# Attention on one core: the inverse softmax sums applied to the probabilities, or to the product with the values

## The reference, cut to what matters

```
q = xn @ w_q.T        # 16 heads of 32
k, v = split(xn @ w_kv.T)             # one key and one value head, shared by the 16
attn = softmax(causal(rotary(q) @ rotary(k).T))
out = (attn @ v, heads side by side) @ w_proj.T + b_proj
shared = relu(xn @ up.T)**2 @ down.T  # 1024 wide
routed = 8 of 32 experts for each token, chosen by groups, weighed, summed
return x + out + shared + routed
```

## Time and profile before

| | |
|---|---|
| median of 3 runs | 1771.65 us (1771.54 to 1773.84) |
| span of the profiled execution | 1784.5 us |
| PE busy of the span | 1640.6 us, 92% |
| DVE busy of the span | 1202.6 us, 67% |
| ACT busy of the span | 1073.5 us, 60% |
| middle, batch 0 | 143.1 to 304.3 us |
| middle, batches 1 to 7 | 304.3 to 1125.4 us |
| experts | from about 1156 us |

### The profile page before, as it was taken

How to read it: one execution, slowest core, us unless ns; L and a number is a source line. 1 busy time by engine, 2 the same in 40 slices (tenths; PEclk the granted TensorE clock), 3 DMA queues, 4 the chain that set the end, 5 groups by cost and what they waited for, 6 DMA issues and landing times.

```text
span 1784.5 us, 40620 instructions
## 1 busy us (share of the span) xinstructions
PE 1640.6 (92%) x10811; PEld 1385.8 (78%) x10811; DVE 1202.6 (67%) x3666; ACT 1073.5 (60%) x2799; POOL 822.7 (46%) x669
## 2 busy tenths in 40 slices
PE   5836779999999999999999999899999999999999
PEld 5835557777777777777777777689999999999987
DVE  7857876877777867767778678355555555555567
ACT  2324545775675756757757667466666666666652
POOL 0032101442443424434424345177777777777760
PEclk9967889999999999999999999999999999999999
DMA  7983242443434434435434344489999999998894
GB/s 283 372 279 88 55 71 79 137 128 101 157 115 144 126 99 131 135 103 153 137 104 133 102 146 122 135 154 184 186 185 195 194 177 197 210 176 159 139 251 187
DMA packets 193666, 277.91 MB, mean 156 GB/s; under 512 B 37464, under 2 KB 133855, under 8 KB 190884
## 3 DMA queue, kind: packets, MB, share of 16 engines
q0 software_dynamic: 60352, 92.59, 23.9%
q1 hardware_dynamic: 78148, 117.20, 23.0%
q10 hardware_dynamic: 54944, 65.52, 12.5%
HBM read 123.93 MB, written 131.76 MB: 143 GB/s over the span
## 4 chain that ended last, share of the span: by engine, by line
PE 63%; DVE 12%; issue 8%; ACT 4%; DMA 3%; POOL 2%; DVEq 1%; SPq 0%; another core or an unknown queue 0%; ACTq 0%; POOLq 0%
PE e_psH L1644 12%; PE e_psY L1655 11%; PE m_psT L1250 6%; PE m_psU L64 4%; DVE m_sc L1047 4%; PE m_psU L66 4%; PE m_psS L1233 4%; PE m_psU L65 4%; PE m_psO L1274 4%; PE e_psX L1629 3%; PE m_psY L66 3%; PE m_psY L64 3%; PE m_psY L65 3%; POOL sums L1609 2%; ACT m_sc L899 2%
## 5 line engine op out<-in xcount | busy, mean ns | idle before, releaser
L1609 POOL DMA_INDIRECT sums<-e_y,e_where x287 | 445.3, 1551 | 156.5 <-issue 94.4
L823 POOL DMA_INDIRECT slot_rows<-m_row,slots x256 | 268.6, 1049 | 501.1 <-ACT m_sc L899 457.2
L899 ACT ACTIVATE m_sc<-m_sc,m_low 128x512 f32<-128x512 f32 (+3 forms) x512 | 283.7, 557 | 173.9 <-DVE m_low L1047 150.8
L1644 PE MATMUL e_psH<-e_xt,e_w_of 128*128 128x128 f32 x2296 | 303.6, 275 | 3.2 <-ACT e_xt L1504 3.2
L1047 DVE CUSTOM_DVE_ANT_0 m_sc<-m_psS,cst 128x512 f32<-128x512 f32 (+3 forms) x512 | 230.0, 485 | 107.0 <-PE m_psS L1233 104.8
L1655 PE MATMUL e_psY<-e_w,e_ht 128*128 x1148 | 295.7, 380 | 2.3 <-ACT e_ht L1515 2.1
L1644 PEld LDWEIGHTS e_psH<-e_xt,e_w_of 128*128 128x128 f32 x2296 | 279.0, 192 | 3.7 <-ACT e_xt L1504 3.5
L1510 ACT ACTIVATE e_w_of<-e_w 128x512 f32 x287 | 180.9, 630 | 120.9 <-issue 119.0
L1250 PE MATMUL m_psT<-cst,m_sc 128*128 128x128 f32 x1280 | 204.1, 280 | 10.5 <-ACT m_pt L910 9.4
L1655 PEld LDWEIGHTS e_psY<-e_w,e_ht 128*128 128x128 f32 x1148 | 196.2, 191 | 18.0 <-issue 3.2
L1233 PE MATMUL m_psS<-m_ks,m_qs 96*128 96x256 f32 (+2 forms) x512 | 156.6, 371 | 57.4 <-DVE m_low L1047 39.8
(11 more groups left out here) (204 smaller groups left out, 3166.1 us busy)
## 6 DMA issues: line engine op xcount, KB each, us to landing
e_row<-slot_rows ACTq DMA_DIRECT2D x287, 144.5 KB
m_qs<-m_qhi SPq DMA_DIRECT2D x256, 64.0 KB
e_w<-in_w SPq DMA_DIRECT2D x256, 64.0 KB
f_xt<-in_x SPq DMA_DIRECT2D x8, 1024.0 KB, 9.5
xnt_hi<-f_hi SPq DMA_DIRECT2D x8, 1024.0 KB, 4.5
xnt_lo<-f_lo SPq DMA_DIRECT2D x8, 1024.0 KB, 8.1
m_qs<-m_qlo SPq DMA_DIRECT2D x128, 64.0 KB
m_res<-in_x SPq DMA_DIRECT2D x8, 1024.0 KB
```

What stands on the lines that cost most here:

```text
L823: pool.indirect_dma_start(out=xs, out_offset=bass.IndirectOffsetOnAxis(ap=slots_sb[:, g, k:k + 1], axis=0), in_=row[g % 2][:, :], in_offse ...
L899: nc.scalar.activation(cols, cols, ACT.Exp, bias=low[:, h % 2, i:i + 1], scale=-1.0, accum_out=total[:, h % 2, i:i + 1]).then_inc(exp_done, 1)
L1609: pool.indirect_dma_start(out=both_sums, out_offset=bass.IndirectOffsetOnAxis(ap=where[u % NY][:, 0:1], axis=0), in_=y[u % NY][:, :], in_o ...
L1644: mm = pe.matmul(psH[u % 2][:, k * P:(k + 1) * P], w1_of[u % 2][:, c * INTER + k * P:c * INTER + (k + 1) * P], xt[u % 2][:, c * P:(c + 1) ...
```

## The change

The probabilities stay unscaled: `scale` keeps only its reciprocal (now `invert`), written so that the inverse sums of four heads lie side by side. Before a group's product with the values, DVE copies these inverses to the part of ot that the group will fill, each repeated over 32 columns (`spread`, 128x512, in slots 4, 8, 12 and 16, between the first two masks and the shared expert's step). PE turns them with four transposes into the bank psU (`inverses`, in slots 5, 9, 13 and 17, ahead of the third row of scores), so that they stand as the product with the values does. ACT copies them back to ot (`copy_inverses`, between its second and third exponentials). When the product is there, DVE multiplies it with them into ot (`normalise`, at the end of the same slot). ACT's `keep` goes; its last step, the high parts for the projection, becomes `highs`. The wait for `tagged_saved` stands now in `spread(1)`, on DVE in slot 8.

```diff
+INV_AT = {HC * _c + HC + 1: _c for _c in range(KC)}
...
-                def keep(c):
+                def copy_inverses(c):
+                    act.wait_ge(u_done, at(b, NU, U_AT[f"inv{c}"] + 1))
+                    nc.scalar.activation(ot[:, c, :], psU[:, :], ACT.Copy).then_inc(inv_copied, 1)
...
-                    if first and c == 1:
-                        act.wait_ge(routing.tagged_saved, 16)
...
-                        dve.wait_ge(scaled, at(b, NH, h - 1))
...
-                def scale(h):
+                def invert(h):
                     dve.wait_ge(exp_done, at(b, NH * TB, TB * (h + 1)))
-                    nc.vector.reciprocal(inv[:, h % 2, :], total[:, h % 2, :]).then_inc(inv_made, 1)
-                    dve.wait_ge(inv_made, at(b, NH, h + 1))
-                    for i in range(TB):
-                        cols = sc[:, h % 2, SPC[i]:SPC[i] + (i + 1) * P]
-                        last = nc.vector.tensor_scalar(cols, cols, inv[:, h % 2, i:i + 1], None, ALU.mult)
-                    last.then_inc(scaled, 1)
+                    nc.vector.reciprocal(inv[:, h // HC % 2, :, h % HC], total[:, h % 2, :]).then_inc(inv_made, 1)
+
+                def spread(c):
+                    dve.wait_ge(inv_made, at(b, NH, HC * (c + 1)))
+                    if first and c == 1:
+                        dve.wait_ge(routing.tagged_saved, 16)
+                    nc.vector.tensor_copy(ot[:, c, :].rearrange("p (k d) -> p k d", d=HD),
+                                          inv[:, c % 2, :, :].rearrange("p i n -> p (i n)").unsqueeze(2).broadcast_to([P, TB * HC, HD])
+                                          ).then_inc(inv_spread, 1)
+
+                def normalise(c):
+                    dve.wait_ge(pv_done, at(b, KC, c + 1))
+                    dve.wait_ge(inv_copied, at(b, KC, c + 1))
+                    nc.vector.tensor_tensor(ot[:, c, :], psO[:, :], ot[:, c, :], ALU.mult).then_inc(o_out, 1)
...
                         mask_and_min(s, ROWS[1])
+                    if s + 1 in INV_AT:
+                        spread(INV_AT[s + 1])
                     if 1 <= s <= NH:
                         shared(s - 1)
...
-                        scale(s)
+                        invert(s)
                     if s - 2 in Q_AT:
                         low_part(b, f"q{Q_AT[s - 2]}")
+                    if s in INV_AT:
+                        normalise(INV_AT[s])
...
                     if g == 0:
-                        pe.wait_ge(scaled, at(b, NH, h + 1))
+                        pe.wait_ge(exp_done, at(b, NH * TB, TB * (h + 1)))
...
+                def inverses(c):
+                    bank_free(b, f"inv{c}")
+                    pe.wait_ge(inv_spread, at(b, KC, c + 1))
+                    for i in range(TB):
+                        mm = pe.transpose(psU[:, i * P:(i + 1) * P], ot[:, c, i * P:(i + 1) * P], ident)
+                    mm.then_inc(u_done, 1)
...
+                    if s in INV_AT:
+                        inverses(INV_AT[s])
                     if s < NH:
                         scores(s, ROWS[2])
                         scores(s, ROWS[3])
```

More of the change, by code:

```diff
@@ L636 @@
 Q_AT = {q_slot(n): n for n in range(1, KC)}
+INV_AT = {HC * _c + HC + 1: _c for _c in range(KC)}
 U_ORDER = []
-for _s in range(NH):
-    U_ORDER.append(f"up{_s}")
+for _s in range(NSLOT):
+    if _s in INV_AT:
+        U_ORDER.append(f"inv{INV_AT[_s]}")
+    if _s < NH:
+        U_ORDER.append(f"up{_s}")
     if _s in Q_AT:
@@ L683, in middle @@
         total = sb("m_total", [P, 2, TB])
-        inv = sb("m_inv", [P, 2, TB])
+        inv = sb("m_inv", [P, 2, TB, HC])
         ot = ot_flat[:, :].rearrange("p (c s) -> p c s", c=KC)
@@ L712, in middle @@
         rot_step, rotated, lo_made, v_made = sem("m_rot_step"), sem("m_rotated"), sem("m_lo_made"), sem("m_v_made")
-        s_out, inv_made, scaled = sem("m_s_out"), sem("m_inv_made"), sem("m_scaled")
+        s_out, inv_made, inv_copied, inv_spread = sem("m_s_out"), sem("m_inv_made"), sem("m_inv_copied"), sem("m_inv_spread")
         sq_made, sqlo_made, res_made, y_out = sem("m_sq_made"), sem("m_sqlo_made"), sem("m_res_made"), sem("m_y_out")
@@ L852, in act_program @@
         def act_program(act, load_first_rows):
-            for s_ in (exp_done, relu_made, sqhi_made, ta_out, tb_out, o_out):
+            for s_ in (exp_done, relu_made, sqhi_made, ta_out, tb_out, inv_copied):
                 act.sem_inc(s_, BASE)
@@ L912, in ta, with highs @@
                         nc.scalar.activation(pt[:, h % HC, 1024:1280], psT[0][:, 0:256], ACT.Copy).then_inc(ta_out, 1)
-                def keep(c):
-                    act.wait_ge(pv_done, at(b, KC, c + 1))
-                    act.wait_ge(y_done, at(b, 4, 0))
-                    if first and c == 1:
-                        act.wait_ge(routing.tagged_saved, 16)
[L920 to L926, removed]
+                def copy_inverses(c):
+                    act.wait_ge(u_done, at(b, NU, U_AT[f"inv{c}"] + 1))
+                    nc.scalar.activation(ot[:, c, :], psU[:, :], ACT.Copy).then_inc(inv_copied, 1)
+                def highs():
+                    act.wait_ge(pv_done, at(b, KC, KC))
+                    act.wait_ge(y_done, at(b, 4, 0))
+                    for k in range(KC):
+                        act.wait_ge(o_out, at(b, KC, k + 1))
+                        nc.scalar.activation(oh[:, k, :], ot[:, k, :], ACT.Copy).then_inc(oh_made, 1)
                 def shared(s):
@@ L939, in batch @@
                     if s < NH:
-                        for i in ROWS:
-                            exps(s, i)
+                        exps(s, ROWS[0])
+                        exps(s, ROWS[1])
+                    if s in INV_AT:
+                        copy_inverses(INV_AT[s])
+                    if s < NH:
+                        exps(s, ROWS[2])
+                        exps(s, ROWS[3])
                     if s == 2 and not first:
@@ L947, in batch @@
                         shared(s)
-                    if s > HC and s % HC == 1:
-                        keep(s // HC - 1)
+                    if s == NSLOT - 1:
+                        highs()
                     if first and PROJ_AT <= s < PROJ_AT + KC:
@@ L988, in dve_program @@
             dve.sem_inc(v_made, BASE - 1)
-            for s_ in (s_out, inv_made, scaled, sq_made, sqlo_made, res_made, y_out):
+            for s_ in (s_out, inv_made, inv_spread, o_out, sq_made, sqlo_made, res_made, y_out):
                 dve.sem_inc(s_, BASE)
@@ L1119, in batch @@
                     dve.wait_ge(oh_made, b * KC + c + 1)
-                    nc.vector.tensor_tensor(ol[:, c, :], psO[:, :] if c == KC - 1 else ot[:, c, :], oh[:, c, :].bitcast(F32),
+                    nc.vector.tensor_tensor(ol[:, c, :], ot[:, c, :], oh[:, c, :].bitcast(F32),
                                             ALU.subtract).then_inc(ol_made, 1)
@@ L1165, in bank_free @@
                     pe.wait_ge(relu_made, at(b, NH, int(last[2:]) + 1))
+                elif last.startswith("inv"):
+                    pe.wait_ge(inv_copied, at(b, KC, int(last[3:]) + 1))
                 elif last == "vt":
```

## The result

The changed kernel takes 1797.95 us (median of 4 runs, 1796.38 to 1799.46), against 1772.74 for the kernel before (4 runs): the ratio is 1.014, interval 1.0126 to 1.0155, slower by 25 us. Forecast were 1800.0 us and +28.4.

What follows compares the result with a forecast made beforehand. PE was taken to bound batches 1 to 7, busy 786.9 of 821.1 us. Batches 1 to 7 at +13.1 and batch 0 at +15.5 gave +28.6, scaled to +28.4: 1800.0 us, range 1782 to 1810.

Steps and rivals of the forecast that it cites:

- Transposes, +12.3: Batches 1 to 7, PE: 28 groups of four transposes at 0.44 us each, no gap to hide in; +12.3 us.
- The copy, +5.3: Batches 1 to 7, DVE: spread delays later masks in slots 4 and 12, 0.38 us in each of 14; +5.3 us.
- Slot 8, -2.0: Batches 1 to 7: DVE's lateness of 0.67 us goes, less the copy's 0.38; -2.0 us in all.
- Slots 3, 7 and 11, -2.5: Batches 1 to 7: low part starts 0.12 us earlier, then waits for ACT's high part; 21 slots, -2.5 us.
- Together +13.1: Sum for batches 1 to 7: 12.3 + 5.3 - 2.0 - 2.5 = +13.1 us.
- Batch 0, +15.5: Batch 0: 13.9 moved wait + 2.0 clock - 0.8 slot 12 + 0.4 slot 17 = +15.5 us.
- the wait and the clock behind it: Batch 0, slot 8: DVE waits for the weights' store, then PE runs 4.0 us at half clock, losing 2.0.
- the 2.0 us of gain ahead of it: Batch 0 before the store's wait: removed scaling wins 2.0 us (ends 0 and 7), bringing the store forward too.
- Rival B: Batch 0: store is down before DVE comes to it; +10.7 us in all, 1782.3 us; chance 0.11.
- C: Batches 1 to 7 come out even, only batch 0's wait counts; +15.5 us, 1787.0 us; chance 0.09.
- D: PE's four transposes don't overlap, 0.28 us each instead of 0.11; +19.0 more, 1818.9 us; chance 0.04.
- Rival A: DVE's relief reaches PE: 35.5 us of mask waits go, batch 0 gains 7; -7.4, 1764.3 us; chance 0.10.

Runs made afterwards that it cites:

- the late copy: Changed kernel with spread moved behind the fourth mask of its slot, ahead of the reciprocal: 1785.17 us, ratio 1.0059.
- the last three experiments: Low part moved behind two masks, with both repairs: 1752.87 us; same move in the kernel before: 1761.97; low part one step sooner than in the first: 1761.61.
- the second trace of before: The kernel before, unchanged, profiled again: span 1773.1 us (first trace 1784.5), timed at 1774.79 us, ratio 1.0001.
- the run with the store sooner: Changed kernel with SP's store of the routing's weights issued ahead of the twelve transfers of queries: 1783.04 us, ratio 1.0046.
- the one with the other tile: Changed kernel with the second group's inverses staged in m_kv, not ot, the store's wait moving to normalise(1) in slot 9: 1782.7 us, ratio 1.0046.
- the doubled transposes: Changed kernel with each of the four transposes of the inverses done twice, into the same place: 1814.57 us, ratio 1.022.
- the one with both repairs: Changed kernel with second group's inverses staged in m_kv and spread moved behind the fourth mask: 1773.14 us, ratio 0.9986.

## Why the prediction was right

The mechanisms came as named; the terms, each against what the runs show:

- Transposes, +12.3: slots 5, 9 and 13 grew by 0.40, 0.40 and 0.38, the batch's end with slot 17 by 0.37 (medians), so 7 x 1.55 = +10.9. The size of a group was right (0.44 in the chain, 0.41 to 0.43 when doubled), and no group found a gap of PE to hide in. The figure of the Trainium skill ("TensorE: Matmul & The Clock Gate", Part 4), 275 ns, is again the length of one (272 ns here), not what one in a row of four adds.
- The copy, +5.3: 0.32 + 0.31 in slots 4 and 12, 7 x 0.63 = +4.4; the late copy gives it back.
- Slot 8, -2.0: 8.40 to 8.10, 7 x 0.30 = -2.1.
- Slots 3, 7 and 11, -2.5: 0.05 + 0.07 + 0.07, so -1.3. That they would hardly shrink, because DVE then waits for ACT's high part, is what the 1.15 us wait and the last three experiments show.
- Together +13.1 forecast; these terms as measured give +11.9. The batch lengths give 7.7 for six batches and at most 1.9 for the seventh and what follows, +9.6. Between them stand two things that the prediction didn't have: the 1.9 us for which PE waits for xlo in this trace of before and not in that of the changed kernel, and slot 2, shorter by 0.09.
- Batch 0, +15.5: +15.1 measured against the second trace of before, +16.8 against the first. The prediction's parts are +17.9 for the wait and the clock behind it (without the gain ahead of the store) and -2.4 for the rest. Measured, the wait cost 17.0 us against the run with the store sooner and 19.4 against the one with the other tile, so the rest of the batch gained 1.9 to 4.3. At a granted clock of 0.50 PE ran for 3.5 us, forecast 4.0. The third mask came at 234.6, forecast 233.3. SP issued the store at 218.65, 0.6 us sooner than in the first trace of before (219.25) and 1.7 sooner than in the second (220.39), so whether the 2.0 us of gain ahead of it came can't be told from these traces. That batch 0 comes out within 0.4 us is partly luck: the two traces of before alone differ by 1.7 there.

Rival B fell with the landing 14.7 us after the issue, C with the 1.3 us by which a batch grew, D with the doubled transposes. Rival A was right in direction: the run without scaling shows 12 us of relief, against the 35.5 us of waits that A counted on. The Trainium skill's advice ("Perfetto Trace Analysis", Optimization Strategies) to optimize the engines that block PE holds in this case, but what to do on DVE is not told by its load: taking 134 us of work off brought 12 us, moving the one step that waited for ACT brought 13 in the kernel before and 20 in the one with both repairs (1773.14 to 1752.87, each beside 1774.89 for the kernel before).

## What to carry to other kernels

An engine that others wait for need not be short of time: look at what its late step waits for when the work ahead of it is gone, and ask whether that step can be moved. Here the move and the lighter load were worth 13 and 12 us alone, and 22 together, with the transposes already paid. A copy or a wait put into an in-order engine is paid for by everything queued behind it, so ask what is the least urgent place in the slot. When a buffer gets a second use, the wait for its first use must move to an instruction with nothing urgent behind it.

## What was not expected of the hardware

- The copy that widens 16 inverse sums to 512 columns by reading each 32 times, took 450 ns on average and 0.34 us from start to start, less than the 507 ns of the multiplication by a column that had been taken as its nearest row.
- The store of 528 KB to rows took 14.7 to 17.0 us to land in the eleven traces in which SP issues twelve transfers of queries just ahead of it, and 14.1 in the one in which it goes ahead of them.
